# Column quarters for the ninth tap, transposes for the offset turns, column halves for logits and pooled sums, and VectorE copies for the last tile's halves

## What is computed

```python
# layer 0: deformable convolution on the group-normalised image
offset = conv3x3(x, offset_w) + offset_b            # 18 offsets for each pixel
x_off  = weighted gathers of x at p0 + pn + offset  # 9 taps, two table rows each
x      = x + conv(x_off, conv_w)
# layer 1: causal attention over the 3136 pixels as tokens, head size 128
t = t + softmax(causal(q k^T / sqrt(128))) v
# layer 2: 64 experts, each takes its best 8 tokens
logits = t_n @ gate_w^T + gate_b                    # 64 x 3136 for each image
vals, idx = top_k(softmax over tokens, 8)
pooled = sum over the 8 chosen tokens of t_n * vals # 64 x 128 for each image
out    = two matmuls per expert on pooled; added back to the chosen tokens
```

## Time and profile before

| | us |
|---|---|
| median of three runs | 2852.54 |
| the profiled execution | 2856.15 |
| its span, first to last instruction | 2854.2 |
| step 0 begins | 61.4 |
| image 0, steps 0 to 24 | 295.9 |
| images 1 to 6, each | 321.2 |
| the steps after 199 until the pooled rows of image 7 are turned | about 121 |
| `second_part` | about 152 |

### The profile page before, as it was taken

How to read it: one execution, slowest core, us unless ns; L and a number is a source line. 1 busy time by engine, 2 the same in 40 slices (tenths; PEclk the granted TensorE clock), 3 DMA queues, 4 the chain that set the end, 5 groups by cost and what they waited for, 6 DMA issues and landing times. The chain is left out here.

```text
span 2854.2 us, 53356 instructions
## 1 busy us (share of the span) xinstructions
PE 2662.3 (93%) x19070; PEld 2079.5 (73%) x19070; DVE 1876.2 (66%) x7203; ACT 1763.3 (62%) x4094; POOL 1763.4 (62%) x1831
## 2 busy tenths in 40 slices
PE   5688999999999999999999999999999998999787
PEld 3466887778777887778877887778777887777564
DVE  3466675876677775866677775876677766765335
ACT  3465666666676666666676666666676667665330
POOL 5777776776577756776577756776577756740000
PEclk8899999999999999999999999999999999999899
DMA  6455334643355324643356324643355323532199
GB/s 190 119 148 138 113 113 128 164 118 99 92 161 143 112 86 125 164 118 93 92 164 145 113 84 125 159 123 96 92 162 152 113 85 103 127 78 97 44 395 392
DMA packets 218354, 382.66 MB, mean 134 GB/s; under 512 B 43865, under 2 KB 128921, under 8 KB 217195
## 3 DMA queue, kind: packets, MB, share of 16 engines
q0 software_dynamic: 88992, 250.76, 31.4%
q1 hardware_dynamic: 126507, 114.05, 13.3%
q10 hardware_dynamic: 2592, 14.45, 1.2%
HBM read 317.00 MB, written 62.13 MB: 133 GB/s over the span
## 5 line engine op out<-in xcount | busy, mean ns | idle before, releaser
L551 POOL DMA_INDIRECT shared<-pair_table,idx x1800 | 1742.9, 968 | 791.4 <-issue 528.8
L1207 PEld LDWEIGHTS bank_o<-vals,prob_t 128*128 128x128 f32 x4800 | 585.4, 192 | 120.3 <-ACT prob_t L598 65.0
L598 ACT ACTIVATE prob_t<-bank_r 128x512 f32<-128x512 f32 (+2 forms) x704 | 369.9, 546 | 464.0 <-PE bank_r L1193 463.2
L1207 PE MATMUL bank_o<-vals,prob_t 128*128 128x128 f32 x4800 | 615.2, 277 | 31.8 <-ACT prob_t L598 31.7
L844 DVE SCALAR_TENSOR_TENSOR shared<-shared,wb 128x128 f32<-128x128 f32 x1800 | 516.9, 347 | 193.0 <-ACT shared L579 192.2
L856 DVE CUSTOM_DVE_ANT_0 prob<-bank_r,mask 128x512 f32<-128x512 f32 (+2 forms) x704 | 432.9, 626 | 267.5 <-PE bank_r L1171 248.6
L579 ACT ACTIVATE shared<-shared,wa 128x128 f32<-128x128 f32 x1800 | 560.8, 391 | 42.7 <-DMA shared<-pair_table,idx 42.7
L1171 PE MATMUL bank_r<-keys,qt 128*128 128x512 f32 (+3 forms) x1344 | 586.9, 554 | 0.0
L1153 PEld LDWEIGHTS bank_r<-convw_t,smp_t 128*128 128x128 f32 x3600 | 443.0, 194 | 57.0 <-issue 37.2
L1153 PE MATMUL bank_r<-convw_t,smp_t 128*128 128x128 f32 x3600 | 476.2, 278 | 1.6 <-ACT smp_t L584 1.6
L1193 PE MATMUL bank_r<-ident,prob 128*128 128x128 f32 x2504 | 368.0, 274 | 4.9 <-ACT prob L677 4.9
(11 more groups left out here) (183 smaller groups left out, 2331.0 us busy)
## 6 DMA issues: line engine op xcount, KB each, us to landing
shared<-in_dram SPq DMA_DIRECT2D x32, 1024.0 KB, 17.9
shared<-pair_table,idx POOLq DMA_INDIRECT x1800
pair_table<-rows_out SPq DMA_DIRECT2D x112, 256.0 KB
t<-in_dram SPq DMA_DIRECT2D x48, 256.0 KB, 4.0
t_dram<-t SPq DMA_DIRECT2D x48, 256.0 KB
shared<-in_dram SPq DMA_DIRECT2D x7, 1568.0 KB
stage<-t_dram POOLq DMA_DIRECT2D x8, 832.0 KB, 7.8
pm_dram<-logit SPq DMA_DIRECT2D x8, 800.0 KB, 8.1
```

What stands on the lines that cost most here:

```text
L551: pool.indirect_dma_start(g[t % RING][:, n, :], None, pair_table[b % 2], bass.IndirectOffsetOnAxis(ap=idx[:, b % 2, i * TAPS + n:i * TAPS ...
L598: act.activation(prob_t[q % 3][:, 0:w], ring_bank(("prob", t, c))[:, 0:w], ACT.Copy)\
L1207: last = pe.matmul(attn_ps, prob_t[q % 3][:, n * P:(n + 1) * P], vals[:, slot(tb, at), :], start=(at == 0), stop=(at == ti))
```

## The change

Five things. (1) The ninth tap of a chunk is done as four matmuls of two rows (112 columns) each, one in each column quarter, in place of one of eight rows. (2) A turn becomes a plain transpose of each tile, four or three tiles to a bank, so there are seven turns an image and not four, two of them one after the other in steps 7, 9 and 11; the four partial sums are added by a DVE reduction that reads PSUM with a stride of 32 elements, and the bias is added by one more DVE instruction in `index_cells`. (3) `logit` is two matmuls of 256 columns in two column halves, with two ACT evictions. (4) `pooled` puts even tiles into the lower column half and odd ones into the upper; a matmul with two stacked identities (`stack`) adds them as it turns. `rz` is copied to the upper partitions. (5) For the last tile the maxima, sums and outputs of the halves are exchanged by DVE copies; the matmuls, their two bank uses and `sel` and `swap_rows` with their loads are gone.

```diff
+TURN_BANK = 4
+TURNS = 2 * (TILES // TURN) + 1
+LAST_ROWS = ROWS_OFF // 4
...
-    (7, "E", "logit", -1, 5), (7, "F", "turn", 1, 0), (7, "M", "chunk", 1, 2), (7, "L", "turn_xf", -1, 6),
+    (7, "E", "logit", -1, 5), (7, "F", "turn", 1, 0), (7, "F", "turn", 1, 1), (7, "M", "chunk", 1, 2), (7, "L", "turn_xf", -1, 6),
...
+def logit_halves(n):
+
+    w = min(CHUNK, N - n * CHUNK)
+    return [(at // (CHUNK // 2), at, min(CHUNK // 2, w - at)) for at in range(0, w, CHUNK // 2)]
...
-                    last = act.activation(logit[:, n * CHUNK:n * CHUNK + w], ring_bank(use)[0:E, 0:w], ACT.Identity,
-                                          bias=gate_bias[:, 0:1])
+                    for h, at, w in logit_halves(n):
+                        last = act.activation(logit[:, n * CHUNK + at:n * CHUNK + at + w],
+                                              ring_bank(use)[E * h:E * (h + 1), 0:w], ACT.Identity,
+                                              bias=gate_bias[E * h:E * (h + 1), 0:1])
...
+                link(dve.tensor_tensor(pos, pos, off_bias[:].unsqueeze(1).broadcast_to(list(pos.shape)), ALU.add))
                 link(dve.tensor_tensor(pos, pos, base[:, tiles, :], ALU.add))
...
-                    last = dve.tensor_tensor(pos_all[:, TURN * n:TURN * n + m, :],
-                                             ring_bank(use)[:, 0:m * 18].rearrange("p (t k) -> p t k", k=18),
-                                             off_bias[:].unsqueeze(1).broadcast_to([P, m, 18]), ALU.add)
+                    last = dve.tensor_reduce(pos_all[:, tiles.start:tiles.stop, :],
+                                             ring_bank(use)[:, 0:len(tiles) * P]
+                                             .rearrange("p (t q k) -> p t k q", q=4, k=OFF_COLS)[:, :, 0:18, :],
+                                             AXX, ALU.add)
...
+            def swap_halves(swapped, given):
+
+                dve.tensor_copy(swapped[0:ROWS_HALF, :], given[ROWS_HALF:, :])
+                link(dve.tensor_copy(swapped[ROWS_HALF:, :], given[0:ROWS_HALF, :]))
...
                     after(exp_done, t + 1)
-                    link(dve.reciprocal(inv_total[:], total[t % 2][:]))
+                    if split(t):
+                        swap_halves(other_sum, total[t % 2])
+                        link(dve.tensor_tensor(inv_total[:], other_sum[:], total[t % 2][:], ALU.add))
+                        link(dve.reciprocal(inv_total[:], inv_total[:]))
+                    else:
+                        link(dve.reciprocal(inv_total[:], total[t % 2][:]))
                     after(attended, t + 1)
-                    add_attention(t, attn_ps)
-                if 0 <= t < ALL and split(t):
-                    after(attended, t + 1)
-                    dve.tensor_copy(both[:, 0:P], attn_ps).then_inc(halved, 1)
+                    if split(t):
+                        swap_halves(other, attn_ps)
+                        link(dve.tensor_tensor(other, other, attn_ps, ALU.add))
+                    add_attention(t, other if split(t) else attn_ps)
...
+                    if split(ts):
+                        link(negated)
+                        swap_halves(other_max, half_max)
+                        negated = dve.tensor_tensor(nmax[ts % 2][:, 0:1], other_max[:], half_max[:], ALU.min)
...
-                        dve.reciprocal(rz[:], rz[:]).then_inc(rz_done, 1)
+                        link(dve.reciprocal(rz[0:E, :], rz[0:E, :]))
+                        dve.tensor_copy(rz[E:, :], rz[0:E, :]).then_inc(rz_done, 1)
...
-                    for k in range(TAPS):
+                    for k in range(TAPS - 1):
...
+                    for q in range(4):
+                        y = n * ROWS_OFF + 2 + q * LAST_ROWS
+                        last = pe.matmul(bank[q * OFF_COLS:(q + 1) * OFF_COLS, q * LAST_ROWS * W:(q + 1) * LAST_ROWS * W]
+                                         .rearrange("o (y x) -> o y x", x=W), offw_t[:, TAPS - 1, :],
+                                         rows[:, y:y + LAST_ROWS, 2:2 + W], start=False, stop=True, skip_group_check=True)
...
-                    for k in range(min(TURN, TILES - TURN * n)):
-                        last = pe.matmul(bank[:, k * 18:(k + 1) * 18], offs[:, k * P:(k + 1) * P], sel[:],
-                                         start=True, stop=True)
+                    for k, tile in enumerate(turned_tiles(n)):
+                        at = tile % TURN * P
+                        last = pe.transpose(bank[:, k * P:(k + 1) * P], offs[:, at:at + P], ident[:])
...
-                    last = pe.matmul(bank[0:E, 0:w], gate_t[:], xf_t[:, 0:w], start=True, stop=True)
+                    for h, at, w in logit_halves(n):
+                        last = pe.matmul(bank[E * h:E * (h + 1), 0:w], gate_t[:], xf_t[:, at:at + w], start=True, stop=True)
...
-                        last = pe.matmul(bank[0:E, 0:C], pm_tok[:, k, :], xf[:, slot(b, k), :],
-                                         start=(k == 0), stop=(k == TILES - 1))
+                        h = k % 2
+                        last = pe.matmul(bank[E * h:E * (h + 1), 0:C], pm_tok[:, k, :], xf[:, slot(b, k), :],
+                                         start=(k < 2), stop=(k >= TILES - 2))
...
-                    last = pe.transpose(bank[:, 0:E], pooled_rows, ident[0:E, 0:E])
+                    last = pe.matmul(bank[:, 0:E], pooled_rows, stack[:], start=True, stop=True)
...
-                def swap_halves():
-                    use = ("swap", ts, 0)
-                    after(half_done, ts // TILES + 1)
-                    free_ring(use)
-                    pe.matmul(ring_bank(use)[:, 0:1], swap_rows[:], half_max[:], start=True, stop=True).then_inc(swapped, 1)
-
-                def merge_halves(t):
-                    use = ("merge", t, 0)
-                    after(halved, t // TILES + 1)
-                    free_ring(use)
-                    pe.matmul(ring_bank(use)[:, 0:P + 1], ident[:], both, start=True, stop=False)
-                    pe.matmul(ring_bank(use)[:, 0:P + 1], swap_rows[:], both, start=False, stop=True).then_inc(merged, 1)
```

More of the change, by code:

```diff
@@ L96 @@
 FIRST_ORDER = (("rows", 0), ("rows", 1), ("rows", 2), ("chunk", 0), ("rows", 3), ("rows", 4), ("chunk", 1), ("turn", 0),
-               ("rows", 5), ("rows", 6), ("setup", 0), ("chunk", 2), ("chunk", 3), ("turn", 1), ("chunk", 4),
-               ("chunk", 5), ("turn", 2), ("chunk", 6), ("turn", 3))
+               ("turn", 1), ("rows", 5), ("rows", 6), ("setup", 0), ("chunk", 2), ("chunk", 3), ("turn", 2), ("turn", 3),
+               ("chunk", 4), ("chunk", 5), ("turn", 4), ("turn", 5), ("chunk", 6), ("turn", 6))
 LOAD_STEP = 15
@@ L105, in misc_at, with turns_after, turned_tiles @@
     return [(what, b + d, n) for t, at, what, d, n in MISC if t == s and at == place and 0 <= b + d < B]
+def turns_after(c):
+    return [n for n in (c - c % 2, c - c % 2 + 1) if n < TURNS]
+def turned_tiles(n):
+    first = TURN * (n // 2) + n % 2 * TURN_BANK
+    return range(first, min(first + TURN_BANK, TURN * (n // 2 + 1), TILES))
 def misc_order():
@@ L113, in misc_order @@
         if c % 2 or c == OFF_CHUNKS - 1:
-            order.append(("turn", 0, c // 2))
+            order += [("turn", 0, n) for n in turns_after(c)]
     for step in range(END):
@@ L182, in ring_order @@
         order += [("score", ts, c) for c in range(min(chunks_in(ts), 3))]
-        order += [("merge", step - LAG_T, 0)] if 0 <= step - LAG_T < ALL and split(step - LAG_T) else []
         order += misc_at(step, "E")
@@ L193, in ring_order @@
             order += misc_at(step, "M") if c == 1 else []
-        order += [("swap", ts, 0)] if 0 <= ts < ALL and split(ts) else []
         order += misc_at(step, "L")
@@ L657, in _ @@
                     act.activation(gate_t[:], ring_bank(("setup", 0, 2))[:, 3 * P:3 * P + E], ACT.Copy).then_inc(setup_ev, 1)
+                    for h in range(2):
+                        act.activation(stack[E * h:E * (h + 1), :], ident[E * h:E * (h + 1), E * h:E * (h + 1)], ACT.Copy)\
+                           .then_inc(stacked, 1)
                 else:
@@ L675, in _ @@
                     row = prob_at(v, 0, width_of(v))
-                    sums = both[:, P:P + 1] if split(v) else total[r][:, 0:1]
-                    act.activation(row, row, ACT.Exp, bias=nmax[r][:, 0:1], accum_out=sums)\
+                    act.activation(row, row, ACT.Exp, bias=nmax[r][:, 0:1], accum_out=total[r][:, 0:1])\
                        .then_inc(exp_done, 1)
@@ L783, in index_cells @@
                 pos, q, cell = views(tiles)[0:3]
-                emptied(after, ("turn", k, 0 if tiles == EARLY_TILES else 3))
-                after(weights_in, 16 * 11)
+                emptied(after, ("turn", k, 1 if tiles == EARLY_TILES else TURNS - 1))
+                after(weights_in, 16 * 10)
+                link(dve.tensor_tensor(pos, pos, off_bias[:].unsqueeze(1).broadcast_to(list(pos.shape)), ALU.add))
```

(15 more changed lines are left out.)

72 lines of the change are left out of this document (31 added, 41 removed), and 6 rows, old and new, of the table MISC.

## The result

The changed kernel takes 2789.07 us (median of 4 runs, 2786.36 to 2789.39) where the kernel before took 2854.3 beside it; the ratio is 0.9769 [0.9752, 0.9786]. The forecast was 2787 us, faster. The profiled execution has a span of 2787.1 us, 67.1 less than before.

What follows compares the result with a forecast made beforehand. PE was taken as the bound, with DVE not far behind in steps 7 to 13. Savings of 66 us from the profiled 2856.15 gave 2790, less 3.6 for the median 2786.5, said as 2787; range 2764 to 2821 us.

Steps and rivals of the forecast that it cites:

- The sum: Whole run: images 1 to 6 53 us, image 0 1.6, image 7 5.5, drain 5, before step 0 0.5; 66 us.
- The prices: PE time each part of the change saves in one image, costed from profile rows; together 11.5 us an image.
- What is kept in steps 7 to 13: Full images: of 5.85 us cut from PE there, 3.1 shortens the span, because DVE is late in some steps.
- DVE's charge: Strided PSUM reductions in the turns: 0.42 us for four tiles, 0.35 for three, 0.5 us more per pair of turns.
- Rival D: Turns of steps 7, 11, 12: strided DVE reduction becomes the pace; at 12 ns an element about 2879 us; chance 0.05.
- Image 0: First image: gathers bound it until step 15, so only four logits gain, 1.6 us.
- The drain: After the last image: logit 0.4, exponent wait and matmul 1.3, merge 0.5, pooled sums about 3; 5 us.
- B: Steps 7 to 13: DVE is never late, so the PE cut there stays; 16 us more, 2770 us; chance 0.17.
- C: PE's present waits grow; only steps without one keep their cut, about 4.5 us an image; 2815 us; chance 0.21.
- Half-width instructions above 0.1 us each: PE's matmuls in column halves: a time above 0.1 us each would prove the forecast wrong.

Runs made afterwards that it cites:

- the last run: Two logit maxima moved into step 9, offsets' bias added once to cell bases, image 0's prologue with row groups first, against the changed kernel: 2785.18 us.

## Why the prediction was right, point by point

- **The sum.** Said 66, the span lost 67.1. Images 1 to 6 gave 58.8 (said 53), image 0 with what lies ahead of it -0.2 (said +2.1), image 7 up to step 24 4.7 (said 5.5), drain and second part 3.9 (said 5). So close a hit is in part luck: the full images gave 6 us more than said and the rest 4 us less, and image 0 alone starts image 1 anywhere within 10 us from one profile to the next.
- **The prices.** Ninth tap 0.54 us (said 0.49), a wide logit 0.42 (0.40), pooled sums 2.75 (2.2), a turn of seven tiles about 0.75 of TensorE (0.7). The nearest row with column tiles carried the tap and the logits within 0.05 us. The pooled sums were mis-sized by 0.5: outside the drain the new form takes (25.9 - 4.55) / 7 = 3.05 us an image where I charged 3.4, two of its instructions at their full time; the row alone, 50 x 0.066 = 3.3, was the better guide. The last 0.15 was not traced.
- **What is kept in steps 7 to 13.** Said 3.1 (the terms listed, 0.85 + 0.7 + 0.5 + 0.7 + 0.15, add up to 2.9), the steps' medians gave 3.7. Steps 7 and 8: said 0.85, got 1.6 - the place, "step 8 is DVE's from end to end", was right, and the stretch has now been measured from both sides. Step 9's turn was kept as said, and its chunk too; the wait of step 10 took 0.36 of step 10's chunk in its stead (0.98 us became 1.34). In step 11 I kept 0.7 of 1.2; all of it counted (1.30), so DVE was not late there, and steps 12 and 13 gave nothing in sum.
- **DVE's charge.** A reduction of four tiles was charged 0.42 us, and two in a row (of four and of three tiles) 0.77; they last 0.75 (the row at 1112.40 above). Rival D, 2.6 us for one, is excluded.
- **The exchange.** Said 0.95 us an image and DVE's part hidden. Undone alone it is worth 0.62: the maxima's round trip in step 5 (0.68) is gained, DVE's part in steps 7 and 8 is not hidden but costs 0.2 net of PE's merge.
- **The steps that failed.** Image 0: I gave it 1.6 us for four logits and 0.5 ahead of it, but its end moves by up to 10 us with the wait for gathers at step 15, and the two profiles show no gain. The drain: I gave the pooled sums 3 us there; the cut is there (7.84 to 4.55) and PE's next wait swallows it, because the second part hangs on the last of the stores, that of `rz`. I had read PE's line there and not SP's.
- **Rivals.** B is excluded by the run with PE work added (0.86 us for nothing in steps 8 and 9); C would have left 4.5 us an image, 10.2 came.
- **A sign set wrong.** "Half-width instructions above 0.1 us each" was to prove the forecast wrong. Its own price of 0.46 us for a logit's four was above that already, and the four that the run with PE work added put into step 20 cost 0.43, 0.11 each.

## What to carry to other kernels

Where an engine that is not the bound works without a gap between two hand-overs, find the two ends of that stretch in its line of time: the bound engine's work inside it is free as long as it fits into that engine's waits, its own work has its full price, and outside it is the reverse; an average discount over the steps misprices both. Adding dummy work to each engine at the same place shows which case holds: 0.86 of 0.878 us against 0.00 of 0.86 here, by the medians of six images. Undoing parts one at a time does not add up where two engines are nearly level, and a cut in the drain is worth nothing until the store that the next part waits for is read.

## What was not expected of the hardware

In full images PE drops to half clock at step 18, or less often at step 13, in some images and not in others. Steps 18 of images 2 and 3 of the changed kernel, and step 13 of image 6 with the turn undone:

```profile
891.08:903.71 12.63, 11.97 (x71) 0.86 0.36 105
1203.76:1214.69 10.93, 10.27 (x71) 1.00 0.34 99
```

```profile
2090.75:2103.56 12.81, 11.88 (x73) 0.87 0.87 138
```

The clock falls from 2.4 to 1.2 GHz for part of the step. Step 18 stands behind step 17, in which PE idles longest of all steps of an image (1.57 us on average); step 13 stands behind step 12 (1.09 us). A drop costs 1.7 us in step 18 and 1.2 to 1.7 in step 13. In the fourteen profiles step 18 has 24 drops and step 13 six, one to five of the six images in twelve profiles and none in two, without a relation to the edit that shows: 2 with the change, 1 before, 5 with the turn undone, 0 in the last run. So total times of two kernels can differ by up to 8 us for this alone, and by up to 10 for the end of image 0. The shortest image, and the medians of the steps but 13 and 18, leave both out and are the better scale for an edit of a microsecond.
